# Layer 0 attention: the output product of a slot is placed behind the turning of the probabilities

## The chip, the cores and the metric

One core of a Trainium2 chip runs the whole program. The metric is the time of one execution in microseconds (us) on the device. TensorE (PE in the rows) does matrix products, VectorE (DVE), ScalarE (ACT) and GpSimd (POOL) do the elementwise work, SyncE (SP) issues transfers. Each engine works through its own queue of instructions in order and waits at semaphores that other engines raise.

## The reference, cut to what matters

The model has two layers, each made of a conditioned attention and a conditioned feed-forward part. The change is in the attention of layer 0, for 4 batches of 512 positions and 16 heads of width 128:

```
q, k, v = (y @ Wq, y @ Wk, y @ Wv), split into heads; q, k = rope(q), rope(k)
o = o_cmp * g_cmp + o_slc * g_slc + o_swa * g_swa      # three softmaxes over the same scores
x = x + o.reshape(b, n, H * HD) @ Wo
```

The input y of each layer comes from a two-way recurrence over the sequence (a "unit" of it is one batch and one chunk of 128 channels), which VectorE computes as scans between the heads' work.

## The kernel before, in words

The function `layer0_attn` works through 4 x 16 = 64 heads, all 512 positions of one at a time. The three softmaxes of a head are joined into one matrix of probabilities, `pt`, so a head takes these steps:

- `project_v` (L1018, 48 products of f16, into the bank `ps_v`) and `project` (L1009, 24 products, q and k into `ps_q`);
- `rope`: VectorE (L1205) and ScalarE (`swap`, L869 and L870) read `ps_q`, GpSimd joins them;
- `scores` (L1028, L1030, L1034) into the three banks `ps`;
- `softmax` on VectorE (first instruction L1220, last four L1257) with the exponentials on ScalarE; its last instruction raises the semaphore `p`;
- `turn` (L1046, 10 transposes of 128 x 128 on TensorE, back into `ps`), copied out by ScalarE into `tt_` (L912, three copies, semaphore `t_sb`);
- `values` (L1056, 8 products of f32, into `ps_o`), the probabilities with v;
- `output` (L1078): for each group of four heads and each quarter `co` of the output's columns, 12 products of f16 into `ps_v`, which VectorE adds to `acc` (L1278, semaphore `acc`).

TensorE's queue is written out by a loop over 66 slots, p = 0 to 65. Slot p handles several heads at once, each at another step: `scores(p - 2)`, `project_v(p - 1)`, `project(p)`, `output(p - 6)`, `turn(p - 2)`, `values(p - 2)`, in this order. A slot therefore begins with the scores of a head and ends with the values of the same head, and the softmax of that head has to be made while TensorE does the products between. The bank `ps_v` is used by `project_v`, emptied by ScalarE (`take_v`), then used by `output` and emptied by VectorE; `project_v` of the next slot waits for that.

VectorE has the same loop: the softmax of head p - 2, with a piece of recurrence work in its middle (`between`), the two rope instructions, then `acc` for `output(p - 6)`, then what the slot's place in a group of four, i = p % 4, asks for: after a slot with i = 1 a `log_sum` (L310), after one with i = 2 a `condition` (L314). A slot with i = 1 or i = 3 begins with two backward scans (L294) ahead of its softmax. ScalarE's loop has `swap(p, 0)`, the copies of `turn`, `swap(p, 1)` in this order.

The lines of TensorE's loop that the change touches:

```
for p in range(LAST):
    ...
    if p < HEADS:
        project(p)
    if output_of(p) is not None:
        pe.wait_ge(s["v_sb"], min(p, HEADS))
        output(output_of(p))
    ...
    if p >= 2:
        turn(p - 2)
        values(p - 2)
```

Of the kernel before, what the change touches and what calls it, by code (L numbers as in the profile page):

```python
# [89 lines left out]
def turned_columns(m):  # L90

    return {0: (0, 0), 1: (1, 0), 3: (1, 384), 2: (2, 0)}[m]
# [298 lines left out]
def layer0_attn(k):  # L391
# [7 lines left out]
    HEADS = B * H0  # L399
    GROUPS = B * CC  # L400
    with ExitStack() as ctx:
        def sb(n, s, dt=F32):
# [52 lines left out]
        s = {n: k.sem("a0_" + n) for n in (  # L455
            "const", "wraw", "w64", "whi", "w_ready0", "w_ready1", "w_kept0", "w_kept1", "rot", "wg_loaded", "wg64", "wg_hi", "wg_lo",
            "x_loaded", "sig_step", "sig", "lsum", "inv", "yf", "yhi", "ylo", "gates_raw", "gates_step",
            "gates_sig", "gates", "qproj", "cosed", "swapped", "roped", "q_sb", "ksum", "q_hi", "k_hi", "qk_lo", "vproj", "v_sb", "scores",
            "nmax", "expd", "cmp_step", "cmp_e", "coef", "p_step", "p", "turned", "t_sb", "pv", "of", "o_hi", "o_lo",
            "router", "y", "logits_ps", "logits", "wo_raw0", "wo_raw1", "wo64", "wo_hi", "wo_lo", "out_ps", "acc", "zeroed")}  # L460
# [8 lines left out]
        def cols(t, j, lo=0, hi=None):  # L469

            bank, c0 = score_columns0(j)
            hi = P * (j + 1) if hi is None else hi
            return t[bank][:, c0 + lo:c0 + hi] if isinstance(t, list) else t[:, bank, c0 + lo:c0 + hi]
# [44 lines left out]
        def slot_of(p):  # L518

            return p // H0, p // G, p % G  # L520
# [5 lines left out]
        def output_of(p):  # L526

            return p - (G + 2) if p >= G + 2 else None
# [31 lines left out]
        with nc.Block() as block:  # L560
# [218 lines left out]
            def _(act):  # L779
# [143 lines left out]
                for p in range(LAST):  # L923
# [19 lines left out]
                    if i == 1 and has_next(p):  # L943
                        nb, _, n = next_at(it)
                        wkv.act_log(act, next_unit(it), 0, nb, n, 0)
# [36 lines left out]
            def _(pe):  # L982
                PARTS = ((0, 0), (0, 1), (1, 0))

                def gates(b):

                    if b:
                        pe.wait_ge(s["acc"], output_of(b * H0 + 1) + 1)
                    else:
                        pe.wait_ge(s["v_sb"], 1)  # L990
                    for t in range(TT):
                        at = TILE_SLOT[t] * 48
                        for c in range(CC):
                            for n, (yp, wp) in enumerate(PARTS):
                                mm = pe.matmul(psv[:, at:at + 48], y16[b % 2][:, yp, c, t * P:(t + 1) * P],
                                               wg16[:, wp, c, :], start=c + n == 0, stop=c == CC - 1 and n == 2)
                    mm.then_inc(s["gates_raw"], 1)
# [15 lines left out]
                def project_v(g):  # L1013
                    b = g // H0
                    for t in range(TT):
                        for c in range(CC):
                            for m, (yp, wp) in enumerate(PARTS):
                                mm = pe.matmul(psv[:, t * D0:(t + 1) * D0], y16[b % 2][:, yp, c, t * P:(t + 1) * P],  # L1018
                                               w16[:, g % 2, wp, 2, c, :], start=c + m == 0, stop=c == CC - 1 and m == 2)
                    mm.then_inc(s["vproj"], 1)  # L1020

                def scores(g):
                    pe.wait_ge(s["qk_lo"], g * 2 + 2)
                    for bank, tiles in BANK_TILES0:
                        for j in tiles:
                            lead = NBLK if bank else 0
                            for m, (qp, kp) in enumerate(PARTS):
                                pe.matmul(cols(ps, j, -lead), q16[:, g % 2, qp, j * P:(j + 1) * P],  # L1028
                                          k16[:, g % 2, kp, NBLK - lead:NBLK + P * (j + 1)], start=m == 0, stop=False)
                            mm = pe.matmul(cols(ps, j, P * j), k.ident_b[:], k.causal_b[:],  # L1030
                                           start=False, stop=True)
                        if bank == 1:
                            for m, (qp, kp) in enumerate(PARTS):
                                mm = pe.matmul(ps[1][:, 0:NBLK], q16[:, g % 2, qp, 3 * P:4 * P], k16[:, g % 2, kp, 0:NBLK],  # L1034
                                               start=m == 0, stop=m == 2)
                        mm.then_inc(s["scores"], 1)

                def turn(g):

                    for bank, tiles in ((0, (0,)), (1, (1, 3)), (2, (2,))):  # L1040
                        if bank == 0:
                            pe.wait_ge(s["p"], g * TT + TT)
                        for m in tiles:
                            _, c0 = turned_columns(m)
                            for j in range(m, TT):
                                mm = pe.transpose(ps[bank][:, c0 + (j - m) * P:c0 + (j - m + 1) * P],  # L1046
                                                  cols(pt, j, m * P, (m + 1) * P), k.ident[:])
                        mm.then_inc(s["turned"], 1)

                def values(g):  # L1050
                    for n, m in enumerate((0, 1, 3, 2)):
                        bank, c0 = turned_columns(m)
                        if n == 0 and g:
                            pe.wait_ge(s["of"], g)
                        pe.wait_ge(s["t_sb"], g * 3 + bank + 1)
                        mm = pe.matmul(pso[:, m * P:], v[:, g % 2, m, :], tt_[:, bank, c0:c0 + T - m * P],  # L1056
                                       start=n == 0, stop=n == TT - 1)
                    mm.then_inc(s["pv"], 1)

                def output(n):  # L1060

                    group, co = divmod(n, CC)
                    c = group % CC
                    if co == 0:
                        pe.wait_ge(s["o_lo"], group * G + G)
                        if group < CC:
                            pe.wait_ge(s["wo_lo"], group * G + G)
                    if n:
                        pe.wait_ge(s["acc"], n)
                    output_heads(n, 0, G)  # L1070

                def output_heads(n, lo, hi):

                    group, co = divmod(n, CC)
                    c = group % CC
                    for h in range(lo, hi):
                        for m, (op, wp) in enumerate(PARTS):
                            mm = pe.matmul(out_bank(n), wo16[:, wp, c, h, co * P:(co + 1) * P], o16[:, group % 2, op, h, :],  # L1078
                                           start=h + m == 0, stop=h == G - 1 and m == 2)
                    if hi == G:  # L1080
                        mm.then_inc(s["out_ps"], 1)
# [10 lines left out]
                for p in range(LAST):  # L1092
                    b, it, i = slot_of(p)
                    if p % H0 == 2 and p < HEADS:
                        gates(b)
                    if p >= 2:
                        scores(p - 2)
                    if 1 <= p <= HEADS:
                        if output_of(p - 1) is not None:
                            pe.wait_ge(s["acc"], output_of(p - 1) + 1)  # L1100
                        if p % H0 == 2:
                            pe.wait_ge(s["gates_step"], b * 2 + 1)
                        project_v(p - 1)
                    if p < HEADS:
                        project(p)
                    if output_of(p) is not None:
                        pe.wait_ge(s["v_sb"], min(p, HEADS))
                        output(output_of(p))
                    if p == HEADS + 1:
                        pe.wait_ge(s["swapped"], HEADS * 2)  # L1110
                        pe.wait_ge(s["o_lo"], HEADS - 1)
                        output_heads(OUTPUTS - 4, 0, G - 1)
                    if p >= 2:
                        turn(p - 2)
                        values(p - 2)
                for n in (OUTPUTS - 3, OUTPUTS - 2):
                    output_heads(n, 0, G - 1)
# [10 lines left out]
            def _(dve):  # L1128
# [152 lines left out]
                for p in range(LAST):  # L1281
                    b, it, i = slot_of(p)
                    if i == 1 and has_next(p):
                        nb, _, n = next_at(it)
                        for m in range(2):
                            wkv.dve_backward(dve, next_unit(it), nb, n, m)
# [1725 lines left out]
```

## Time and profile before

| what | value |
|---|---|
| median of 3 runs (lowest, highest) | 2194.34 us (2188.91, 2197.18) |
| the profiled execution | 2195.33 us |
| its span, first to last instruction | 2193.6 us |
| TensorE busy, share of the span | 1919.4 us, 87% |
| VectorE busy | 1594.1 us, 73% |
| ScalarE busy | 1364.2 us, 62% |
| GpSimd busy | 1112.0 us, 51% |
| mean granted clock of TensorE | 0.950 of full speed |

The profiled execution's own time is 1.7 us over its span and 1 us over the median of the runs. Busy shares are means over all stages; the slots of layer 0 take the first half of the span, from about 82 us to 1137 us.

### The profile page before, as it was taken

What the parts mean: (1) busy time and instruction counts of PE and PEld (TensorE: products, weight loads), DVE (VectorE), ACT (ScalarE), POOL (GpSimd) and SP (SyncE); (2) the same over time, 40 slices, a digit from 0 to 9 for tenths busy, and PEclk for the clock granted to TensorE, in tenths of its full rate; (3) what the DMA queues carried; (4) which work ended last, traced back from release to release, by engine and by line L of the source; (5) the groups of instructions that cost most, each with busy time, mean ns of one, the idle gap of its engine ahead of it and who ended that gap; (6) DMA issues with size and microseconds to landing.
All of it is one profiled execution on the core that took longest, in us unless ns stands there. A gap on an engine that the chain in (4) does not pass through costs nothing. (4 is left out here: it accounts for less than half of the span.)

```text
span 2193.6 us, 40174 instructions
## 1 busy us (share of the span) xinstructions
PE 1919.4 (87%) x14497; PEld 1197.4 (55%) x14497; DVE 1594.1 (73%) x3508; ACT 1364.2 (62%) x3321; POOL 1112.0 (51%) x868
## 2 busy tenths in 40 slices
PE   0789999999999999999984999656899888878999
PEld 0456566666656666666664555334556566633444
DVE  7799988888878886888741789546778787734770
ACT  6578776776777777777741343255768686745442
POOL 5677677677667676566613466433223222200540
PEclk9899999999999999999985999878999999889999
DMA  4334432322223222443116644454324243335100
GB/s 175 128 111 135 127 107 76 109 72 81 75 88 101 71 85 83 130 145 118 52 58 260 263 145 148 181 183 131 131 92 147 91 138 128 121 125 190 36 24 19
DMA packets 110977, 256.72 MB, mean 117 GB/s; under 512 B 10944, under 2 KB 39744, under 8 KB 108736
## 3 DMA queue, kind: packets, MB, share of 16 engines
q1 hardware_dynamic: 91520, 204.92, 28.1%
q10 hardware_dynamic: 16704, 40.90, 5.3%
q0 software_dynamic: 2560, 8.39, 1.0%
q8 instruction: 114, 1.87, 0.4%
q14 instruction: 79, 0.65, 0.1%
HBM read 175.79 MB, written 75.24 MB: 114 GB/s over the span
## 5 line engine op out<-in xcount | busy, mean ns | idle before, releaser
L1009 PE MATMUL ps_q<-a_y,a_w 128*128 128x512 f16 x1536 | 343.9, 381 | 57.5 <-POOL a_y L704 57.1
L1009 PEld LDWEIGHTS ps_q<-a_y,a_w 128*128 128x128 f16 x1536 | 147.8, 98 | 225.4 <-issue 60.1
L727 POOL TENSOR_TENSOR a_rb<-a_rb,router_y 128x512 f32<-128x512 f32 x128 | 181.0, 1414 | 167.1 <-ACT a_rb L870 166.4
L1220 DVE TENSOR_REDUCE a_nmax<-ps_s 128x1 f32<-128x512 f32 (+3 forms) x256 | 123.5, 483 | 106.7 <-PE ps_s L1030 106.5
L1018 PE MATMUL ps_v<-a_w,a_y 128*128 128x128 f16 x3072 | 183.1, 220 | 0.0
L869 ACT ACTIVATE a_rb<-ps_q 64x512 f32<-64x512 f32 x128 | 76.0, 593 | 170.4 <-DVE a_ra L1205 168.8
L1056 PE MATMUL ps_o<-a_tt_,a_v 128*128 128x512 f32 (+3 forms) x512 | 158.4, 453 | 24.4 <-ACT a_tt_ L912 21.1
L1018 PEld LDWEIGHTS ps_v<-a_w,a_y 128*128 128x128 f16 x3072 | 175.4, 98 | 1.2
L1078 PE MATMUL ps_v<-a_o,a_wo 128*128 128x512 f16 x732 | 168.0, 379 | 1.9 <-ACT a_v L896 1.9
L889 ACT ACTIVATE ps_s<-ps_s,a_nmax 128x512 f32<-128x512 f32 (+3 forms) x256 | 125.2, 489 | 39.4 <-DVE a_nmax L1222 39.3
L2167 ACT ACTIVATE a_t<-ps 128x512 f16<-128x512 f32 (+1 forms) x192 | 88.0, 525 | 88.7 <-PE ps L2358 79.4
L1028 PE MATMUL ps_s<-a_k,a_q 128*128 128x512 f16 (+3 forms) x768 | 134.0, 304 | 8.3 <-POOL a_k L738 8.3
L736 POOL TENSOR_TENSOR a_q<-a_q 128x512 f16<-128x512 f32 x64 | 75.5, 1180 | 127.3 <-ACT a_q L903 127.3
L2160 ACT ACTIVATE a_ef<-ps,a_nmax 128x512 f32<-128x512 f32 (+3 forms) x256 | 131.7, 537 | 11.7 <-DVE a_nmax L2513 10.3
L1056 PEld LDWEIGHTS ps_o<-a_tt_,a_v 128*128 128x128 f32 x512 | 84.3, 195 | 88.0 <-issue 54.2
L214 POOL TENSOR_TENSOR wkv_eukv<-wkv_euk,wkv_kt 128x512 f32<-128x512 f32 x56 | 76.5, 1366 | 107.1 <-DVE wkv_euk L251 107.1
L1250 DVE SCALAR_TENSOR_TENSOR a_pt<-ps_s,a_coef,a_pc 128x512 f32<-128x512 f32 (+3 forms) x256 | 123.3, 544 | 2.2
L2037 POOL TENSOR_TENSOR a_qk<-a_qkf,a_qk 128x512 f16<-128x512 f32 x32 | 37.1, 1161 | 171.2 <-ACT a_qk L2139 94.3
L2858 PE MATMUL psf_e<-f_h,f_w 128*128 128x512 f16 x512 | 112.7, 382 | 10.0 <-ACT w_w L2793 10.0
L1078 PEld LDWEIGHTS ps_v<-a_o,a_wo 128*128 128x128 f16 x732 | 71.5, 98 | 88.0 <-ACT a_v L896 2.1
L2513 DVE TENSOR_REDUCE a_nmax<-ps 128x1 f32<-128x512 f32 (+3 forms) x256 | 107.3, 477 | 9.0 <-PE ps L2348 8.9
L2519 DVE TENSOR_TENSOR a_t<-ps,a_t 128x512 f16<-128x512 f32 (+1 forms) x192 | 103.5, 589 | 11.4 <-ACT a_t L2167 11.0
(327 smaller groups left out, 4963.0 us busy)
## 6 DMA issues: line engine op xcount, KB each, us to landing
a_w<-wqkv_split SPq DMA_DIRECT2D x48, 768.0 KB, 4.7
scratch_numlog<-wkv_nl ACTq DMA_DIRECT2D x40, 512.0 KB, 2.7
wkv_kt<-in_fT ACTq DMA_DIRECT2D x56, 256.0 KB, 2.9
router_y<-in_wqkv SPq DMA_DIRECT2D x16, 768.0 KB, 5.4
wqkv_split<-a_w SPq DMA_DIRECT2D x16, 768.0 KB, 7.0
a_stacks<-qk_parts SPq DMA_DIRECT2D x96, 128.0 KB, 2.6
gate_up<-in_gate_up SPq DMA_DIRECT2D x8, 1408.0 KB, 11.5
a_nlc<-scratch_numlog SPq DMA_DIRECT2D x18, 512.0 KB, 5.0
```

What stands on the lines that cost most here:

```text
L727: pool.tensor_tensor(rb[:, n, :], rb[:, n, :], rot[:, 2 * n + 1, :], ALU.mult).then_inc(s["roped"], 1)
L889: act.activation(cols(ps, j), cols(ps, j), ACT.Exp, bias=nmax[:, 0, j:j + 1], accum_out=sums[:, 1, n:n + 1]).then_inc(s["expd"], 1)
L1009: mm = pe.matmul(psq[n][:], w16[:, g % 2, wp, n, c, :], y16[b % 2][:, yp, c, :], start=c + m == 0, stop=c == CC - 1 and m == 2)
L1018: mm = pe.matmul(psv[:, t * D0:(t + 1) * D0], y16[b % 2][:, yp, c, t * P:(t + 1) * P], w16[:, g % 2, wp, 2, c, :], start=c + m == 0, stop= ...
L1028: pe.matmul(cols(ps, j, -lead), q16[:, g % 2, qp, j * P:(j + 1) * P], k16[:, g % 2, kp, NBLK - lead:NBLK + P * (j + 1)], start=m == 0, sto ...
L1056: mm = pe.matmul(pso[:, m * P:], v[:, g % 2, m, :], tt_[:, bank, c0:c0 + T - m * P], start=n == 0, stop=n == TT - 1)
L1078: mm = pe.matmul(out_bank(n), wo16[:, wp, c, h, co * P:(co + 1) * P], o16[:, group % 2, op, h, :], start=h + m == 0, stop=h == G - 1 and m ...
L1220: dve.tensor_reduce(nmax[:, 0, j:j + 1], cols(ps, j), AX, ALU.max, negate=True)
L1250: dve.scalar_tensor_tensor(out=cols(pt, j).rearrange("p (m n) -> p m n", n=BLK), in0=cols(ps, j).rearrange("p (m n) -> p m n", n=BLK), sca ...
L2160: act.activation(cols(ef[:, i % 2], j), cols(ps[i % 2], j), ACT.Exp, bias=nmax[:, i % 2, j:j + 1], accum_out=sums[:, i % 2, j:j + 1]).then ...
L2513: m = dve.tensor_reduce(nmax[:, i % 2, j:j + 1], cols(ps[i % 2], j), AX, ALU.max, negate=True)
L2858: mm = pe.matmul(pse[co % 2][:], w1[:, part, co, n, :], h[:, n, :], start=n + part == 0, stop=n == NF - 1 and part == 1)
```

## The change

`output` of a slot is issued between `turn` and `values` instead of ahead of `turn`. No instruction is added or removed, and the waits of each step stay with it.

```
                     if p < HEADS:
                         project(p)
-                    if output_of(p) is not None:
-                        pe.wait_ge(s["v_sb"], min(p, HEADS))
-                        output(output_of(p))
                     if p == HEADS + 1:
                         pe.wait_ge(s["swapped"], HEADS * 2)
                         pe.wait_ge(s["o_lo"], HEADS - 1)
                         output_heads(OUTPUTS - 4, 0, G - 1)
                     if p >= 2:
                         turn(p - 2)
+                    if output_of(p) is not None:
+                        pe.wait_ge(s["v_sb"], min(p, HEADS))
+                        output(output_of(p))
+                    if p >= 2:
                         values(p - 2)
```

This is TensorE's queue in the second half of a slot in the steady state, before (`a0_p`, `a0_t_sb`, `a0_acc` are the semaphores named above; `ident` is the unit matrix of the transposes):

```order
L1009 MATMUL ps_q<-a_y_0,a_w 128x512 [waits a0_swapped]
L1009 MATMUL ps_q<-a_y_0,a_w 128x512 x11
L1078 MATMUL ps_v<-a_o,a_wo 128x512 [waits a0_acc,a0_v_sb]
L1078 MATMUL ps_v<-a_o,a_wo 128x512 x11
L1046 MATMUL ps_s<-ident,a_pt 128x128 [waits a0_p]
L1046 MATMUL ps_s<-ident,a_pt 128x128 x9
L1056 MATMUL ps_o<-a_tt_,a_v 128x512 [waits a0_t_sb,a0_of]
```

And the same place in the changed kernel:

```order
L1009 MATMUL ps_q<-a_y_0,a_w 128x512 [waits a0_swapped]
L1009 MATMUL ps_q<-a_y_0,a_w 128x512 x11
L1046 MATMUL ps_s<-ident,a_pt 128x128 [waits a0_p]
L1046 MATMUL ps_s<-ident,a_pt 128x128 x9
L1078 MATMUL ps_v<-a_o,a_wo 128x512 [waits a0_acc,a0_v_sb]
L1078 MATMUL ps_v<-a_o,a_wo 128x512 x11
L1056 MATMUL ps_o<-a_tt_,a_v 128x512 [waits a0_t_sb,a0_of]
```

The ten transposes, with their wait for the probabilities, now stand directly behind the projections, and the twelve products of `output` stand between them and the values.

On VectorE the order is as it was. This is what stands there around the instruction that takes the output product, in a slot with i = 0 and the start of the next one:

```order
L1257 SCALAR_TENSOR_TENSOR a_pt<-ps_o,a_coef,a_pt 128x128 [waits a0_p_step]
L1205 TENSOR_TENSOR a_ra<-ps_q,router_y 128x512 [waits a0_q_sb,a0_qproj] x2
L1263 SCALAR_TENSOR_TENSOR a_w<-router_y,a_w 128x1536 [waits a0_whi]
L1278 SCALAR_TENSOR_TENSOR a_acc<-ps_v,a_acc 128x512 [waits a0_acc_loaded2,a0_out_ps]
L1268 SCALAR_TENSOR_TENSOR a_wo<-router_y,a_wo 128x512 [waits a0_wo_hi]
L294 SCALAR_TENSOR_TENSOR wkv_bwd<-ps_d,wkv_tail,wkv_fwd 128x512 [waits wkv0_num,wkv0_ln,wkv0_tail]
L294 SCALAR_TENSOR_TENSOR wkv_bwd<-ps_d,wkv_tail,wkv_fwd 128x512
L1220 TENSOR_REDUCE a_nmax<-ps_s 128x1 [waits a0_scores]
```

Nothing moved here; L1278 waits for the product's end (`a0_out_ps`), and the backward scans and the next softmax are queued behind it (L1263 and L1268 are weight work of the first 15 slots only).

## Rows read from the trace of the kernel before

**Rows 1.** Busy in 154:1102: length, PE, PEld, DVE, ACT, POOL, PEclk, DMA, GB/s.

```profile
154.00:1102.00 948.00, 927.53 (x7161) 583.00 (x7160) 797.52 (x2093) 700.84 (x1831) 656.21 (x515) 1.00 0.30 98
```

**Rows 2.** Waits of TensorE in 154:1102: us in total, times, longest.

```profile
PE ps_o L1056 <- ACT a_tt_ L912: 16.3, 32, 1.2
PE ps_s L1046 <- DVE a_pt L1257: 0.9, 1, 0.9
```

**Rows 3.** Timeline of TensorE, slot p = 40 (i = 0): start, us, engine, line.

```profile
714.55 0.81 PE L1028 MATMUL ps_s<-a_k,a_q 128*128 128x512 f16 x3
...
724.37 2.75 PE L1078 MATMUL ps_v<-a_o,a_wo 128*128 128x512 f16 x12
726.96 1.25 PE L1046 MATMUL ps_s<-ident,a_pt 128*128 128x128 f32 x10
728.48 2.40 PE L1056 MATMUL ps_o<-a_tt_,a_v 128*128 128x512 f32 x8 [0.27 <-ACT a_tt_ L912]
730.72 0.81 PE L1028 MATMUL ps_s<-a_k,a_q 128*128 128x512 f16 x3
```

**Rows 4.** Timeline of VectorE, the same slot.

```profile
715.46 0.69 DVE L1220 TENSOR_REDUCE a_nmax<-ps_s 128x1 f32<-128x512 f32 x1 [3.62 <-PE ps_s L1030]
...
725.55 0.35 DVE L1257 SCALAR_TENSOR_TENSOR a_pt<-ps_o,a_coef,a_pt 128x128 f32<-128x128 f32 x1
...
727.16 0.69 DVE L1278 SCALAR_TENSOR_TENSOR a_acc<-ps_v,a_acc 128x512 f32<-128x512 f32 x1
727.77 2.45 DVE L294 TENSOR_TENSOR_SCAN wkv_bwd<-ps_d,wkv_tail,wkv_fwd 128x512 f32<-128x512 f32 x2
```

**Rows 5.** Timeline of ScalarE, the same slot.

```profile
727.74 1.36 ACT L912 ACTIVATE a_tt_<-ps_s 128x512 f32<-128x512 f32 x3
```

**Rows 6.** Timeline of TensorE, the first products of slots p = 39 and p = 42.

```profile
698.53 0.81 PE L1028 MATMUL ps_s<-a_k,a_q 128*128 128x512 f16 x3
...
746.74 0.81 PE L1028 MATMUL ps_s<-a_k,a_q 128*128 128x512 f16 x3
```

**Rows 7.** Timeline of VectorE and GpSimd, slots p = 38 to 41.

```profile
695.59 1.84 DVE L314 SCALAR_TENSOR_TENSOR a_yf<-wkv_nl,wk_fomd,a_sg 128x512 f32<-128x512 f32 x1
695.61 1.27 POOL L727 TENSOR_TENSOR a_rb<-a_rb,router_y 128x512 f32<-128x512 f32 x1 [3.69 <-ACT a_rb L870]
...
697.35 2.45 DVE L294 TENSOR_TENSOR_SCAN wkv_bwd<-ps_d,wkv_tail,wkv_fwd 128x512 f32<-128x512 f32 x2
...
699.72 0.66 DVE L1220 TENSOR_REDUCE a_nmax<-ps_s 128x1 f32<-128x512 f32 x1
...
709.11 0.35 DVE L1257 SCALAR_TENSOR_TENSOR a_pt<-ps_o,a_coef,a_pt 128x128 f32<-128x128 f32 x1
...
740.99 0.34 DVE L1257 SCALAR_TENSOR_TENSOR a_pt<-ps_o,a_coef,a_pt 128x128 f32<-128x128 f32 x1
```

**Rows 8.** Timeline of VectorE and TensorE, slot p = 4, which has no output product.

```profile
129.34 0.35 DVE L1257 SCALAR_TENSOR_TENSOR a_pt<-ps_o,a_coef,a_pt 128x128 f32<-128x128 f32 x1
...
129.74 1.31 PE L1046 MATMUL ps_s<-ident,a_pt 128*128 128x128 f32 x10 [1.42 <-DVE a_pt L1257]
132.27 2.40 PE L1056 MATMUL ps_o<-a_tt_,a_v 128*128 128x512 f32 x8 [1.22 <-ACT a_tt_ L912]
```

**Rows 9.** Timeline of TensorE, slot p = 11.

```profile
249.44 1.31 PE L1046 MATMUL ps_s<-ident,a_pt 128*128 128x128 f32 x10 [0.94 <-DVE a_pt L1257]
251.98 4.08 PE L1056 MATMUL ps_o<-a_tt_,a_v 128*128 128x512 f32 x8 [1.23 <-ACT a_tt_ L912]
```

**Rows 10.** Busy time during those values, columns as in rows 1.

```profile
252.20:255.60 3.40, 3.40 (x7) 1.77 (x7) 1.73 (x3) 1.58 (x4) 3.32 (x3) 0.50 0.92 217
```

**Rows 11.** Timeline of TensorE, slot p = 65.

```profile
1126.58 2.40 PE L1046 MATMUL ps_s<-ident,a_pt 128*128 128x128 f32 x10 [3.54 <-DVE a_pt L1257]
```

**Rows 12.** Timeline of TensorE and VectorE, slot p = 52 (last batch, i = 0).

```profile
909.83 0.81 PE L1028 MATMUL ps_s<-a_k,a_q 128*128 128x512 f16 x3
...
919.62 0.35 DVE L1257 SCALAR_TENSOR_TENSOR a_pt<-ps_o,a_coef,a_pt 128x128 f32<-128x128 f32 x1
```

More of the change, by code:

```diff
@@ L1105, in _ @@
                         project(p)
-                    if output_of(p) is not None:
-                        pe.wait_ge(s["v_sb"], min(p, HEADS))
-                        output(output_of(p))
                     if p == HEADS + 1:
@@ L1114, in _ @@
                         turn(p - 2)
+                    if output_of(p) is not None:
+                        pe.wait_ge(s["v_sb"], min(p, HEADS))
+                        output(output_of(p))
+                    if p >= 2:
                         values(p - 2)
```

## The prediction, made before the changed kernel ran

> **What bounds the kernel now.** I read the busy time by stage first. In the slots that have both a projection and an output product (p = 6 to 63, 58 slots) TensorE is busy 927.5 of 948.0 us at full granted clock, VectorE 797.5 [rows 1]: TensorE bounds this stage, with 20.5 us of gaps to win at most. The chain of waits says what the gaps are: 16.3 us in 32 waits of the values for ScalarE's copies of the turned probabilities, and only 0.9 us, once, in the turning for the probabilities themselves [rows 2]. So the product that stands between the projection and the turning hides something, and the values are hardly covered.
>
> The timeline of one slot shows what is hidden. I count from the slot's first product, 714.55. The projection is done, and the output product starts, at +9.82; the turning starts at +12.41, the values at +13.93, the next slot at +16.17 [rows 3]. On VectorE the softmax starts at +0.91, when the first scores are there, and its last instruction ends at 725.55 + 0.35 = 725.90, which is +11.35 [rows 4]. The probabilities are thus 1.53 us late for the end of the projection and 1.06 us early for the turning where it now stands. The softmax cannot run ahead: its input is made at the start of the same slot.
>
> **The change, step by step.** No work is added; each slot gets another wait.
>
> The turning, new place. Slot p = 4 has no output product and so already has the order projection, turning: the probabilities end at 129.69 and the turning starts at 129.74, 0.05 later, after 1.42 us without work, and takes 1.31 [rows 8]. I take 0.05 and 1.31 for the new slots.
>
> The product, new place. It takes 2.75 us, and each run's end as shown lies 0.16 beyond the start of the next (724.37 + 2.75 against 726.96) [rows 3]. The values' wait goes: without cover it is 1.22 us [rows 8], now there are 2.59 us of product. ScalarE's three copies take 1.36 us and end 3.2 us after the probabilities (727.74 + 1.36 against 725.90) [rows 4, 5]; the values will start 0.05 + 1.31 + 2.75 - 0.32 = 3.79 us after them, so nothing waits.
>
> The slot's new length is then the end of the probabilities plus 0.05 + 1.31 + 2.75 + 2.40 - 3 x 0.16 = 6.03 us. For i = 0: 11.35 + 6.03 = 17.38 against 16.17, +1.21. For i = 2 the rows repeat: +1.2. For i = 1 (p = 41) the end is 741.33 - 730.72 = +10.61 [rows 3, 7], so 16.64 against 746.74 - 730.72 = 16.02 [rows 6], +0.62. For i = 3 (p = 39) it is 709.46 - 698.53 = +10.93, so 16.96 against 16.02, +0.94 [rows 3, 6, 7].
>
> What is late next: VectorE's take of the product, and what is queued behind it. After the probabilities it does two rope instructions and then waits for the product, which will end 0.05 + 1.31 - 0.16 + 2.75 = 3.95 us after them; L1278 follows 0.04 later, and the instruction behind it starts 0.61 after that [rows 4], at 4.60. The next softmax could start at 6.03 + 0.91 = 6.94. After a slot with i = 0 the two backward scans lie between, 2.37 from start to start (697.35 to 699.72) [rows 7]: 6.97, just late, +0.03. After one with i = 2 there is `condition` too, 1.76 from start to start [rows 7]: 8.73, so 1.79 late, where it is now 699.72 - 698.53 - 0.91 = 0.28 late [rows 6, 7]. That pushes the softmax of the i = 3 slots back by 1.51 more, and their probabilities with it: 0.94 + 1.51 = +2.45. For i = 1: +0.65.
>
> The duration of `condition` is the uncertain price in this. It took 1.84 us beside a multiplication of GpSimd that began 0.02 us after it [rows 7]; L1278, the same kind of instruction on the same 128 x 512 but with one operand in PSUM, took 0.69 [rows 4]. With 0.69 the push is 1.15 less. GpSimd's multiplication follows ScalarE's swap, which follows the rope, so it keeps its place relative to the probabilities and another piece of it will be running; I take 1.84. The Trainium skill (SBUF — State Buffer, on the port pair that VectorE and GpSimd share) has an exclusive lock for a VectorE instruction with two operands in SBUF against a GpSimd instruction that reads SBUF; the rows agree, as the instruction ends 0.55 us after the multiplication.
>
> Sum of the loop: 15 slots each with i = 2 and 3, 14 each with i = 0 and 1: 15 x 1.2 + 15 x 2.45 + 14 x 1.21 + 14 x 0.65 = 80.8. In the last batch the i = 0 slots have no recurrence of a next batch in their softmax: it ends at 919.97 - 909.83 = +10.14 [rows 12], which would make +0.15 and not +1.21 in four slots; I take 3 off, since VectorE will be late there as well: **78**. The slots p = 64 and 65 wait for their probabilities already (3.54 us in the last [rows 11]); there the product only moves from ahead of that wait to behind it, 2 x 2.59 = **5**.
>
> The clock. The longest new stops are those of i = 3: 10.93 + 1.51 + 0.05 - 9.82 = 2.7 us, 15 times; the others are 0.8 to 1.6. In this stage the granted clock is full [rows 1], but after the two stops of slot p = 11 (0.94 and 1.23 us around a turning) it was 0.50, that is 1.2 GHz, and the values took 4.08 us for 2.40 [rows 9, 10], 1.68 more; slot p = 4 with stops of 1.42 and 1.22 kept 2.40 [rows 8]. So a stop of that order sometimes costs 1.7. I take 9 of the 15: 9 x 1.68 = **15**; the ends are none (0) and all 15 with the two last slots (29). The Trainium skill (TensorE: Matmul & The Clock Gate, on oscillation) speaks against this change: activity holds the clock up, and a loop whose engine stops in every turn can pay for the fall in every turn. By that every slot would pay; slot p = 11 agrees and slot p = 4 does not.
>
> Sum: 78 + 5 + 15 = 98 us on the profiled execution's 2195.3 gives 2293; the runs' median is 1 us lower, which I leave.
>
> **Rivals.** *VectorE is not late.* If `condition` and the scans hid behind TensorE, the i = 3 slots would cost 0.94 only: 15 x 1.51 = 23 less, and their stops would be 1.2 us with few falls: 2195 + 55 + 5 = 2255. VectorE does idle 3.62 us ahead of a softmax [rows 4], which speaks for it; the count of 1.79 us above speaks against.
>
> *The clock holds.* Without falls 2195 + 83 = 2278; slot p = 4 speaks for it, p = 11 against.
>
> *The clock falls in most slots*, the page's case: 58 slots and the two last, 60 x 1.68 = 101; 83 + 101 = 184, 2379 at the extreme. The stops of 0.8 to 1.6 us stand alone in a slot, unlike those of p = 11, so I hold it unlikely.
>
> *The other side: the probabilities are in time.* Then each slot wins the values' waits, 16.3 us [rows 2], and 58 times the 0.16 of overlap, 9.3: 2170. It needs probabilities at +9.8 or earlier; a slot loses from about +10.0 on. The earliest that I found is +10.14 [rows 12], most are 0.5 to 1.3 later, and the softmax, bound to its scores, has no reason to end earlier. That order and waits are as the diff says shows in TensorE's queue, so no change at all needs gain and loss to cancel.
>
> **How the numbers follow.** Forecast (probabilities late, VectorE pushed, some falls) 0.60, 2293; its own range 2278 to 2310. The clock holds 0.15; VectorE not late 0.13; most slots fall 0.08; in time 0.02; cancelled 0.02. With the cheap `condition` and no fall the sum is 83 - 15 x 1.15 = 66, so 2261; the other end, all long stops with falls, is 83 + 29, 2307, and a little of the next case. The range 2258 to 2318 leaves out part of VectorE not late (2255), most of the many falls and the last two. A measurement of this kernel can tell about 0.5%, 11 us. Slower 0.96, within 0.02, faster 0.02.
>
> **What would show it.** In the changed profile TensorE should wait for the probabilities in L1046 in nearly every slot, some 80 to 100 us in all where it was 0.9; the waits of L1056 for ScalarE should be gone; L1278 should wait some 2.6 us for TensorE in every slot; slots should take 17.4, 18.5, 17.4 and 16.7 us for i = 2, 3, 0, 1; the softmax of i = 3 should begin 2.7 us after its slot and not 1.19. The granted clock of the stage should be below 1. I am wrong if the probabilities end earlier in their slot than now, if the i = 3 slots stay under 17.2, or if falls come after stops of 1.4 us.

## The result, and the profile after

The changed kernel takes 2296.34 us (median of 4 runs, 2295.6 to 2299.55) against 2194.12 us (4 runs, 2188.91 to 2197.18). The ratio of the two is 1.0471, with a 95% interval of 1.0449 to 1.0494: it is slower by 102 us, where 98 were forecast. The profiled execution took 2296.71 us with a span of 2295.0; the instructions are the same in number, and the difference lies in the slots of layer 0.

The busy time of the slots p = 6 to 63 of the changed kernel, columns as in [rows 1]:

```profile
154.00:1202.00 1048.00, 952.77 (x7164) 592.95 (x7162) 799.30 (x2093) 700.96 (x1831) 656.01 (x519) 0.97 0.27 89
```

The same work takes 1048 us instead of 948. TensorE's busy time rose by 25 us with the same matrix instructions, and its mean granted clock fell to 0.97; the other 75 us are time in which it does nothing.

The waits of TensorE and the two longest of VectorE in this stretch (us in total, times, longest), which answer to [rows 2]:

```profile
PE ps_s L1046 <- DVE a_pt L1258: 95.2, 58, 3.7
...
DVE a_acc L1279 <- PE ps_v L1078: 175.5, 58, 4.5
DVE a_nmax L1221 <- PE ps_s L1030: 37.0, 26, 2.2
```

The turning waits for the last probabilities in each of the 58 slots, 95.2 us where it was 0.9 once, and the values' waits for ScalarE, 16.3 us before, are gone. VectorE now stands 175.5 us in front of the product that it must take. (VectorE's line numbers are one higher than before, L1258 for L1257.)

The timeline of TensorE shows slots p = 38 (i = 2), 39 (i = 3) and the start of 40: start, us, engine, line, in brackets the idle time before and who ended it.

```profile
735.73 0.81 PE L1028 MATMUL ps_s<-a_k,a_q 128*128 128x512 f16 x3
...
747.13 1.31 PE L1046 MATMUL ps_s<-ident,a_pt 128*128 128x128 f32 x10 [1.41 <-DVE a_pt L1258]
748.27 2.75 PE L1078 MATMUL ps_v<-a_o,a_wo 128*128 128x512 f16 x12
750.87 2.32 PE L1056 MATMUL ps_o<-a_tt_,a_v 128*128 128x512 f32 x8
753.02 0.81 PE L1028 MATMUL ps_s<-a_k,a_q 128*128 128x512 f16 x3
...
765.52 1.41 PE L1046 MATMUL ps_s<-ident,a_pt 128*128 128x128 f32 x10 [2.52 <-DVE a_pt L1258]
766.73 4.38 PE L1078 MATMUL ps_v<-a_o,a_wo 128*128 128x512 f16 x12
770.95 2.32 PE L1056 MATMUL ps_o<-a_tt_,a_v 128*128 128x512 f32 x8
773.11 0.81 PE L1028 MATMUL ps_s<-a_k,a_q 128*128 128x512 f16 x3
```

Each slot stops ahead of L1046, 1.41 us for i = 2 and 2.52 for i = 3, and then runs through. In the second slot the turning and the product, which had stood still before, take 1.41 and 4.38 us and not 1.31 and 2.75: 1.73 more. Slot 38 is 753.02 - 735.73 = 17.29 long, slot 39 is 20.09; before they were 16.16 and 16.02.

The timeline of VectorE in the same stretch, and of GpSimd beside `condition` (L314), which answer to [rows 7]:

```profile
746.73 0.35 DVE L1258 SCALAR_TENSOR_TENSOR a_pt<-ps_o,a_coef,a_pt 128x128 f32<-128x128 f32 x1
...
751.07 0.69 DVE L1279 SCALAR_TENSOR_TENSOR a_acc<-ps_v,a_acc 128x512 f32<-128x512 f32 x1 [2.80 <-PE ps_v L1078]
751.67 1.73 DVE L314 SCALAR_TENSOR_TENSOR a_yf<-wkv_nl,wk_fomd,a_sg 128x512 f32<-128x512 f32 x1
753.33 2.45 DVE L294 TENSOR_TENSOR_SCAN wkv_bwd<-ps_d,wkv_tail,wkv_fwd 128x512 f32<-128x512 f32 x2
755.70 0.66 DVE L1221 TENSOR_REDUCE a_nmax<-ps_s 128x1 f32<-128x512 f32 x1
...
765.13 0.34 DVE L1258 SCALAR_TENSOR_TENSOR a_pt<-ps_o,a_coef,a_pt 128x128 f32<-128x128 f32 x1
...
771.15 0.69 DVE L1279 SCALAR_TENSOR_TENSOR a_acc<-ps_v,a_acc 128x512 f32<-128x512 f32 x1 [4.48 <-PE ps_v L1078]
...
751.58 1.28 POOL L727 TENSOR_TENSOR a_rb<-a_rb,router_y 128x512 f32<-128x512 f32 x1
```

After the rope VectorE waits 2.80 us for the product, and only then come `condition`, the two backward scans and the softmax of slot 39, which starts 755.70 - 753.02 = 2.68 us after its slot (1.19 before). Its probabilities end at +12.45 (10.93 before). In slot 38 they end at +11.35, as before.

The granted clock during the long product of slot 39, columns as in [rows 1], which answers to [rows 10]:

```profile
766.60:770.00 3.40, 3.40 (x11) 1.28 (x9) 0.06 (x1) 3.22 (x7) 2.55 (x3) 0.50 0.39 159
```

It is 0.50, that is 1.2 GHz, after a stop of 2.52 us. In this stage such a fall of the clock is seen 17 times (once before), and each costs 1.44 to 1.74 us.

Set against the slots of before, one by one, the 58 slots are 99.3 us longer, the last two 7.5, the first four 0.3 shorter: 106.5. The span grew by 101.4 only; the other 5 us lie outside these slots, where no instruction was changed.

### The profile page after: what moved, and what is told of

It reads as the page before. It is cut to its first block and busy times, and to the rows that moved or that the text cites. A ratio compares the mean times of both kernels' runs of the same rounds, so it can differ in the third digit from the quotient of the medians.

```text
span 2295.0 us, 40174 instructions
## 1 busy us (share of the span) xinstructions
PE 1944.5 (85%) x14497; PEld 1206.3 (53%) x14497; DVE 1596.1 (70%) x3508; ACT 1364.1 (59%) x3321; POOL 1107.3 (48%) x868
## 5 line engine op out<-in xcount | busy, mean ns | idle before, releaser
L1078 PE MATMUL ps_v<-a_o,a_wo 128*128 128x512 f16 x732 | 191.9, 418 | 0.0
L1046 PE MATMUL ps_s<-ident,a_pt 128*128 128x128 f32 x640 | 93.2, 298 | 111.8 <-DVE a_pt L1258 111.8
L1279 DVE SCALAR_TENSOR_TENSOR a_acc<-ps_v,a_acc 128x512 f32<-128x512 f32 x61 | 42.2, 692 | 187.5 <-PE ps_v L1078 187.5
L1056 PE MATMUL ps_o<-a_tt_,a_v 128*128 128x512 f32 (+3 forms) x512 | 152.8, 442 | 4.5 <-ACT a_tt_ L912 4.5
L1046 PEld LDWEIGHTS ps_s<-ident,a_pt 128*128 128x128 f32 x640 | 75.4, 150 | 143.1 <-DVE a_pt L1258 143.1
L1078 PEld LDWEIGHTS ps_v<-a_o,a_wo 128*128 128x128 f16 x732 | 78.7, 108 | 91.3 <-issue 31.3
```

## The experiments

Three edits of the changed kernel test the three terms of the sum; the rest asks what the old place is worth, and whether a better one exists. "Before" is the kernel before, measured on the same chip as each run. The "take" is VectorE's instruction that adds the product to `acc` (L1279); "steady" are the slots whose lengths repeat every four slots, mainly those of the two middle batches.

**VectorE's queue.** What the take held up is put ahead of it: `log_sum` and `condition`, and the backward scans of the next slot (`backward`, which stood at the start of that slot).

```diff
-                    if output_of(p) is not None:
-                        output(output_of(p))
                     if late_piece(p) is not None:
                         scaled_wo_low(late_piece(p))
...
                     if late_of(p - 2) is not None:
                         late_condition(late_of(p - 2))
+                    backward(p + 1)
+                    if output_of(p) is not None:
+                        output(output_of(p))
```

> The changed kernel, with one change on VectorE: the condition step and the next slot's two backward scans are issued ahead of the instruction that takes the output product, so the late product holds up nothing. If the late product is what pushes the softmax of the i = 3 slots (the prediction's step), that softmax starts 0.9 us after its slot and not 2.7, its probabilities end at about +10.6, the slot takes 10.6 + 6.0 = 16.6 us and not 18.4 to 20.1, its stop is 0.8 us with no clock fall behind it, and the i = 1 slots lose 0.3 us too: 15 x 2.6 + 14 x 0.3 = 43 us less than the changed kernel, about 2253. If the softmax of those slots is late for another reason, the time stays at 2290 to 2300.

It took 2246.93 us (2240.96 to 2247.29), 1.0236 of before (1.0214 to 1.0257), 49 us less than the changed kernel. VectorE in the same place of that kernel, slot 39 starting at 725.20:

```profile
718.90 0.34 DVE L1258 SCALAR_TENSOR_TENSOR a_pt<-ps_o,a_coef,a_pt 128x128 f32<-128x128 f32 x1
...
720.36 0.74 DVE L314 SCALAR_TENSOR_TENSOR a_yf<-wkv_nl,wk_fomd,a_sg 128x512 f32<-128x512 f32 x1
721.02 2.45 DVE L294 TENSOR_TENSOR_SCAN wkv_bwd<-ps_d,wkv_tail,wkv_fwd 128x512 f32<-128x512 f32 x2
723.39 0.66 DVE L1279 SCALAR_TENSOR_TENSOR a_acc<-ps_v,a_acc 128x512 f32<-128x512 f32 x1
726.10 0.69 DVE L1221 TENSOR_REDUCE a_nmax<-ps_s 128x1 f32<-128x512 f32 x1 [2.05 <-PE ps_s L1030]
```

And TensorE there:

```profile
725.20 0.81 PE L1028 MATMUL ps_s<-a_k,a_q 128*128 128x512 f16 x3
...
736.23 1.31 PE L1046 MATMUL ps_s<-ident,a_pt 128*128 128x128 f32 x10 [1.04 <-DVE a_pt L1258]
737.37 2.75 PE L1078 MATMUL ps_v<-a_o,a_wo 128*128 128x512 f16 x12
...
742.12 0.81 PE L1028 MATMUL ps_s<-a_k,a_q 128*128 128x512 f16 x3
```

The softmax starts 0.90 after its slot, and now waits for its scores. The steady i = 3 slots come down from 20.08 to 16.92, and of 17 falls of the clock 2 are left. So the push through VectorE's queue is real, and the falls hang on it. The waits for the probabilities remain:

```profile
153.30:1146.70 993.40, 927.98 (x7164) 583.23 (x7163) 773.98 (x2093) 702.89 (x1831) 652.53 (x519) 1.00 0.29 94
...
PE ps_s L1046 <- DVE a_pt L1258: 65.4, 58, 2.5
```

Which of the moved instructions counts, the next run tells: only `log_sum` and `condition` go ahead of the take, and the scans stay in the next slot.

```diff
-                    if output_of(p) is not None:
-                        output(output_of(p))
                     if late_piece(p) is not None:
...
                     if late_of(p - 2) is not None:
                         late_condition(late_of(p - 2))
+                    if output_of(p) is not None:
+                        output(output_of(p))
```

> The changed kernel with only the condition step (and the log sums) ahead of VectorE's take of the product; the backward scans stay behind it. The push of the i = 3 slots was counted as the condition step's 1.66 us; the scans alone were counted as 0.03 late. So i = 3 should begin its softmax at +1.0 like i = 1, and take 16.9: within 8 us of the run with both moved, 2247 to 2255. If the scans are the larger part of the push, 2270 or more.

2249.18 us (2247.69 to 2249.92), 1.0253 of before (1.0237 to 1.0269), against 1.0236 with the scans ahead too: the softmax of i = 3 starts at +1.02 and the slot takes 16.93. For the i = 3 slots `condition` behind the take is nearly the whole push.

**The clock.** Six products of the same kind, whose result is overwritten, fill part of the stop.

```diff
+                    if output_of(p) is not None and p < HEADS:
...
+                        for m in range(6):
+                            pe.matmul(psv[:], wo16[:, 0, group % CC, 0, 0:P], o16[:, group % 2, 0, 0, :],
+                                      start=m == 0, stop=m == 5)
```

> The changed kernel with six more products of 128 x 512 between projection and turning in the slots p = 6 to 63, which work on operands at hand and whose result is overwritten. They take 1.37 us. If the clock falls come from the length of the stop, the i = 3 stops shrink from 2.7 to 1.3 us and no fall is left in the loop: 17 falls of 1.7 us (29 us) less, and about 6 us more where the probabilities end before the six products do: about 2273. If the falls have nothing to do with the stops, 2296 + 6 = 2302.

2283.73 us (2279.66 to 2290.5), 1.0422 of before (1.0399 to 1.0444): a kernel with 348 more products takes 13 us less. TensorE in its slot 39, which starts at 737.67:

```profile
747.49 1.46 PE L1114 MATMUL ps_v<-a_o,a_wo 128*128 128x512 f16 x6
750.17 1.31 PE L1046 MATMUL ps_s<-ident,a_pt 128*128 128x128 f32 x10 [1.22 <-DVE a_pt L1268]
751.32 2.75 PE L1078 MATMUL ps_v<-a_o,a_wo 128*128 128x512 f16 x12
...
756.06 0.81 PE L1028 MATMUL ps_s<-a_k,a_q 128*128 128x512 f16 x3
```

The probabilities end as late as in the changed kernel (+12.44), but the product takes 2.75 and the slot 18.39: the difference to 20.08, 1.7 us, is the clock alone. 2 falls of 17 are left. The loop became 17.9 us shorter, where 15 falls at 1.7 are 25.5, so the filler took 7.6 back: about 5 where the probabilities were nearly in time, for which 6 were expected, and 2.7 in slots 51 and 59, whose softmax begins later. The gain was smaller than the 23 us expected by the two falls that stayed and this second part, and by the spread of the runs, whose median lies 4 us over the profiled execution (2279.66).

**The lateness of the probabilities.** In the i = 0 and i = 2 slots both forward scans of the recurrence go from the middle of the softmax to behind the rope.

```diff
-                        if i == 0 and has_next(p):
...
-                            wkv.dve_forward(dve, next_unit(it), nb, n)
...
                         rope(p, 1)
+                    if i == 0 and has_next(p):
...
+                        wkv.dve_forward(dve, next_unit(it), nb, n)
...
```

> The changed kernel, with the two forward scans of the i = 0 and i = 2 slots issued behind the probabilities and the rope, where VectorE waits for the output product anyway. If a slot's length is set by the end of its probabilities, these end at +10.1 and not at +11.35 in about 25 slots, and such a slot takes 16.1 and not 17.3: 30 us less, about 2266 (falls of the clock may come elsewhere, 10 us either way). If the slot is set by TensorE or ScalarE and the end of the probabilities only looks like the releaser, the time stays at 2296.

2277.8 us (2275.86 to 2285.37), 1.0396 of before (1.0372 to 1.042). TensorE in slot 38, at 725.67:

```profile
735.87 1.31 PE L1046 MATMUL ps_s<-ident,a_pt 128*128 128x128 f32 x10 [0.21 <-DVE a_pt L1258]
...
741.76 0.81 PE L1028 MATMUL ps_s<-a_k,a_q 128*128 128x512 f16 x3
```

The probabilities end 1.20 us earlier (+10.14), and the slot is 1.20 shorter, 16.09: its length is their end plus 5.95, in this kernel and in the changed one (11.34 and 17.29). The i = 0 and i = 2 slots together give 40 us, four falls of the clock included; the scans, now behind the rope, push the i = 1 and i = 3 slots by 13, falls of the clock (10 in this kernel) included. The expected time was 12 us too low, by that push.

**A part of the product in each place.** Three of the four heads stay ahead of the turning, one goes behind it, so that it covers the values' wait as well. On the kernel before:

```diff
-                        output(output_of(p))
+                        output(output_of(p), 3)
...
                         turn(p - 2)
+                    if output_of(p) is not None:
+                        output_heads(output_of(p), 3, G)
+                    if p >= 2:
                         values(p - 2)
```

> The kernel before with the output product split: three heads ahead of the turning, the fourth behind it, nothing else moved. The turning can start at +11.76, which is behind the probabilities in all slots but a few, so by the step of the late probabilities nothing is lost there; but VectorE takes the product some 1.1 us later. If a later product pushes the i = 3 softmax also in this small form, its probabilities end at about +12.4 and 15 slots take 17.2 for 16.0; i = 1 gains 0.3, i = 0 and 2 nearly nothing (ScalarE's copies wait for swap(p, 0)): about 2204. If cover behind the turning is all that counts, every slot gains 0.28: 2178.

2191.47 us (2185.92 to 2195.52), 0.9983 of before (0.9969 to 0.9997): neither number. The i = 1 slots go from 16.02 to 15.66 and the i = 3 slots to 15.75, but i = 0 and i = 2 stay at 16.16: there ScalarE starts the copies of the turned probabilities at +13.19 as before, so the values cannot start earlier. The push that I had expected did not come in the steady slots either, since `condition` took 0.76 us (in the last batch it did: slots 51, 55 and 59 take 16.9 for 16.02):

```profile
689.82 1.27 POOL L727 TENSOR_TENSOR a_rb<-a_rb,router_y 128x512 f32<-128x512 f32 x1 [3.69 <-ACT a_rb L870]
...
690.88 0.76 DVE L314 SCALAR_TENSOR_TENSOR a_yf<-wkv_nl,wk_fomd,a_sg 128x512 f32<-128x512 f32 x1
```

An earlier run brings the copies forward as well, ahead of ScalarE's first swap, and has the take last (the cut shows the swap alone):

```diff
-                    if p < HEADS:
-                        swap(p, 0)
                     if p >= 2:
                         turn(p - 2)
+                    if p < HEADS:
+                        swap(p, 0)
```

> The kernel before, with the output product split: the products of three heads ahead of the turning, those of the fourth behind it; ScalarE's copies of the turned probabilities ahead of swap(p, 0); and VectorE's take of the product behind the condition step and the next backward scans. By my sum the turning starts at +11.76, when all probabilities but a few are there, the last 0.65 us of the product cover the copies, and a slot takes 15.75 us: 0.28 less in the 29 slots that take 16.02 now and 0.42 in those of 16.17, about 20 us, so 2174. If the values' wait isn't coverable (the copies come as late as before), 2190 to 2195; if the three queues' new order delays something else, over 2195.

2228.86 us (2227.07 to 2234.65), 1.0167 of before (1.0149 to 1.0186): 55 us over my sum, the expectation's last case. The later swap makes GpSimd's rope later, GpSimd's next work is the recurrence's, and VectorE waits for that in the middle of a softmax:

```profile
703.16 1.47 DVE L251 TENSOR_SCALAR wkv_euk<-wkv_ek_raw,wk_eu,wk_cap 128x512 f32<-128x512 f32 x1 [2.40 <-POOL wkv_nl L233]
```

The probabilities of the i = 1 and i = 3 slots end at +13.9 instead of 10.6, and those slots take 17.93. I had costed the move on ScalarE alone. With the swap back in its place, the split and the take last:

> The split of three heads and one, and VectorE's take of the product behind the condition step and the backward scans, with swap(p, 0) in its old place ahead of the copies. If it was the late swap that spoiled the version with the copies first (GpSimd's rope, then its join, then VectorE's euk), the probabilities of i = 1 and 3 end at +10.6 again and these 29 slots take 15.72 for 16.02, the others 16.13 for 16.17: 9 us less than before, 2183. If the take was what spoiled it, over 2220.

2184.82 us (2180.61 to 2190.25), 0.995 of before (0.9931 to 0.997), as expected: it was the late swap. And the take last alone, on the kernel before:

> The kernel before with VectorE's take of the product behind the condition step and the backward scans, as in the run with the change, and nothing else. The i = 3 softmax then starts 0.9 and not 1.19 us after its slot, but its probabilities are 1.5 us early for the turning already: no difference, 2190 to 2194. If this order is worth something by itself, the 50 us that it brought in the changed kernel would partly show here as well (2170 or less).

2191.21 us (2186.62 to 2196.02), 0.9985 (0.9973 to 0.9998): with the product in its old place VectorE's order is worth next to nothing, where in the new place it was worth 49 us.

**The rest of the probabilities' way.** Added to the split with the take last: both forward scans of the i = 0 slots behind the rope,

> The version with the split and the take moved, and also the forward scans of the i = 0 slots behind their probabilities. Those end at +10.1 and not at +11.35, swap(p, 0) and the copies come 1.2 us earlier, and some 11 slots with i = 0 take 15.72 for 16.17: 13 us less than before, about 2178. If VectorE then comes late to the next softmax by more than the 1.1 us that the i = 1 slots have to spare, the gain is gone: 2185 or more.

2191.96 us (2185.23 to 2195.31), 0.9982 (0.9968 to 0.9996): the second case of the expectation. The i = 0 slots take 15.66, but the softmax of the i = 1 slots starts 2.01 after its slot, and they take 16.62. Then the second of the two scans alone, for i = 0 and i = 2:

```diff
-                            wkv.dve_forward(dve, next_unit(it), nb, n)
+                            wkv.dve_forward_ek(dve, next_unit(it), nb, n)
...
                         rope(p, 1)
+                    if i == 0 and has_next(p):
...
+                        wkv.dve_forward_ekv(dve, next_unit(it), nb, n)
```

> The version with the split and the take moved, and the second of the two forward scans of the i = 0 and i = 2 slots (1.2 us, with the small instruction behind it) issued behind the probabilities and the rope. If the end of the probabilities sets when ScalarE swaps and copies, they end at about +10.2 in these slots, the values start at +13.5 and not +13.93, and with one scan only VectorE is back in time for the next softmax: some 26 slots take 15.66 for 16.16, 13 us less than without it, and 24 less than before: about 2170. If VectorE comes late again, as with both scans behind, 2185 or more.

2181.27 us (2179.72 to 2185.7), 0.9943 (0.9929 to 0.9957), between the two numbers. All steady slots take 15.66, but some of the first and the last batch, where VectorE has more to do (p = 7, 9, 11, 15, 51, 55, 59), take 16.9 to 21.2. The same two edits of VectorE with the whole product in the changed kernel's place:

> The changed kernel's place of the product with the same two edits on VectorE (take behind the condition step and the backward scans, second forward scan behind the probabilities). VectorE then pushes nothing and the probabilities end at about +10.2 in i = 0 and 2 and +10.97 in i = 1 and 3. By the prediction's sum of 5.95 a slot still takes 16.15 and 16.92, since the probabilities are never there at +9.8: about 2247 - 28 = 2219, some 25 us more than before. If the place itself costs nothing once VectorE is in order, at most 2195.

2229.34 us (2228.44 to 2234.06), 1.017 (1.0155 to 1.0186), 48 us more than with the split and 10 more than expected: the steady slots are 16.09 and 16.93, as worked out, some of the first batch over 19. Even with VectorE's order made for it, the place behind the turning costs. Last, the split everywhere, and the two edits of VectorE only in p = 16 to 47 (the cut is against the version with both edits everywhere):

```diff
+                    late_take = H0 <= p < 3 * H0
...
+                    if not late_take and output_of(p) is not None:
+                        output(output_of(p))
...
-                    backward(p + 1)
-                    if output_of(p) is not None:
+                    if late_take:
+                        backward(p + 1)
                         output(output_of(p))
```

> The split of the output product in all slots, and the two edits on VectorE (take behind the condition step and the backward scans, second forward scan behind the probabilities) only in the slots p = 16 to 47; in the first batch VectorE has weight work and in the last one the late recurrence work, and there the version with both edits everywhere had i = 3 slots of 16.9 to 21.2. The 32 slots keep their 15.66, 17 us less than before, the others go as in the version with the split alone, near zero: about 2176. If the edits bring nothing beyond the version with the take alone, 2185.

2177.95 us (2176.26 to 2180.8), 0.9933 of before (0.9919 to 0.9947): 15 us faster than before. Its slots p = 6 to 63, and TensorE in one of them:

```profile
154.20:1085.10 930.90, 918.39 (x7164) 583.82 (x7163) 790.91 (x2093) 703.18 (x1831) 656.64 (x516) 1.00 0.31 100
...
693.14 2.11 PE L1078 MATMUL ps_v<-a_o,a_wo 128*128 128x512 f16 x9
695.09 1.25 PE L1046 MATMUL ps_s<-ident,a_pt 128*128 128x128 f32 x10
696.18 0.81 PE L1078 MATMUL ps_v<-a_o,a_wo 128*128 128x512 f16 x3
696.83 2.32 PE L1056 MATMUL ps_o<-a_tt_,a_v 128*128 128x512 f32 x8
```

No idle time stands in brackets any more: nine products cover the probabilities, three the copies. Of 20.5 us of gaps before, 12.5 remain; the rest of the gain is in the busy time, 918.39 for 927.53 us [rows 1].

## Why the prediction was right, and where its sizes were off

The mechanism was the one forecast, but that the sum came out so close (98 for 101.4 of span) is in part luck: one term was 12 us too high, three were 20.5 too low together, and 5 us fell away elsewhere.

**The waits: 43 us, not 55.** The first kernel of the experiments has only these: 44.8 us in the loop, less one fall more than before (1.7). Step by step the rule holds: slot = end of the probabilities + 5.95 (6.03 was worked out; the values take 2.32, not the 2.40 of [rows 3]), steady slots +1.13 for i = 0 and 2 and +0.90 for i = 1 and 3. What was too high is the number of slots to which it applies. I took 3 us off for the last batch and for i = 0 alone; there the i = 3 slots too have early probabilities, and with VectorE's order mended both kinds cost +0.07. Nor did I see that some slots of before were late already: p = 11 took 19.97 there, 17.23 in that experiment.

One cost I had at nothing. I took over the end of the probabilities from the kernel before, but in i = 1 it moved from +10.61 to +10.97. In the first experiment the softmax starts where it did, at +0.90, and one of its last instructions, whose `a_ewn` and `a_pt` both lie in SBUF, takes 1.24 us and not 0.41. These are slot 41 of before and slot 37 of that experiment:

```profile
740.66 0.41 DVE L1257 SCALAR_TENSOR_TENSOR a_pt<-a_ewn,a_coef,a_pt 128x192 f32<-128x192 f32 x1
740.77 1.33 POOL L738 TENSOR_TENSOR a_k<-a_kk,a_k 128x520 f16<-128x520 f32 x1
...
700.32 1.16 POOL L738 TENSOR_TENSOR a_k<-a_kk,a_k 128x520 f16<-128x520 f32 x1
700.46 1.24 DVE L1258 SCALAR_TENSOR_TENSOR a_pt<-a_ewn,a_coef,a_pt 128x192 f32<-128x192 f32 x1
```

Before, GpSimd's instruction began 0.11 us behind it and took 1.33; now it begins 0.14 ahead of it and takes 1.16. Earlier instructions of the softmax give 0.47 of the 0.83 back, and 0.36 remain: with the 0.08 less of the values, the +0.62 that I had for i = 1 becomes +0.90. In i = 3 it hardly shows, because the softmax there starts 0.29 earlier than before. In the changed kernel itself the instruction takes 1.15 in i = 1 and 0.97 in i = 3.

**The push: 29 us, not 23.** In the i = 3 slots it was 23.4, as worked out: softmax at +2.68 (2.7 forecast), slot 18.39 without the clock (18.47 forecast). For the other slots I had almost none; the i = 1 slots lost 3.3 us and the i = 2 slots 2.3 by a late VectorE, in part in the last batch (p = 53 and 61: +1.71, of which 0.65 and 0.63 remain with the take last). The uncertain price, `condition`, was 1.73 for the 1.84 that I took, and the rival in which VectorE is not late is refuted by the start of the softmax and by two experiments.

**The clock: 27 us, not 15.** 17 falls and not 9, 12 of them in i = 3 slots, the others in p = 9, 18, 34, 50 and 58. In the changed kernel 17 of the 20 stops of 2.08 us or more were followed by a fall, and none of the 38 shorter ones, of which 1.41 us is the usual length; so falls after stops of 1.4, which I had named as a sign of error, did not come. This is a count and no limit: in the kernel before the clock fell after stops of 0.94 and 1.23 us [rows 9], and with the filler it did not after one of 2.46 us (p = 11). The filler shows that the stop is the cause: with the same late probabilities and TensorE at work in half of the stop, 2 falls were left. The Trainium skill (TensorE: Matmul & The Clock Gate, on oscillation) says that a loop which stops in every turn can pay in every turn; the trace agrees for the long stops, which pay every fourth slot, and not for the 1.41 us stops. That the same stop of 2.51 us was followed by a fall in p = 34 and not in p = 18 of the first experiment stays unexplained, and so does why 17 fell and not 9.

**The last two slots: 7.5 us, not 5.** The product moved behind a wait as said, but the clock fell too, where I had reckoned with full speed. TensorE in slots 64 and 65, to be read against [rows 11]:

```profile
1212.20 2.40 PE L1046 MATMUL ps_s<-ident,a_pt 128*128 128x128 f32 x10 [5.39 <-DVE a_pt L1258]
1214.39 4.13 PE L1078 MATMUL ps_v<-a_o,a_wo 128*128 128x512 f16 x12
...
1230.70 2.35 PE L1046 MATMUL ps_s<-ident,a_pt 128*128 128x128 f32 x10 [5.26 <-DVE a_pt L1258]
1232.84 3.44 PE L1078 MATMUL ps_v<-a_o,a_wo 128*128 128x512 f16 x12
```

In slot 64 turning and product take 2.47 us more than the usual 1.31 and 2.75, in slot 65 the product 0.69 more; its turning was slow before as well.

**Outside the slots: 5 us less, not forecast.** No cause was found. In the experiments' profiles the same difference between the slots' sum and the span is -3.5 to +3.2 us, with the same code there, so most of it may be the spread of those stages; that is not shown.

The signs: the turning's waits were 95.2 us (80 to 100 forecast), ScalarE's waits gone, the slots 17.29, 18.39 and the clock, 17.29, 16.92 (17.4, 18.5, 17.4, 16.7). VectorE's wait for the product is 2.80 us in steady slots (2.6 forecast) and 3.0 on average, as the slow products lengthen it. The rival that ends faster needed probabilities at +9.8; none came before +10.14 in a steady slot, as in [rows 12].

## What to carry to other kernels

A product that stands ahead of a wait is paid for by that wait: before it is moved, count when the awaited operand is ready against the end of what would then precede it, because a wait of 0.9 us in the profile can hide one of 95. Then look at who takes the moved result on an engine that works in order; here what was queued behind the take cost 29 us and the stops that this made longer most of 27 more in clock, and one reordering of that queue gave back half of the loss. Where two waits each need a part of the cover, split the product, and price such an edit in every queue that it delays: the split, with VectorE's order fitted to it, gave 0.7%, and its version that held up one swap on ScalarE lost 1.7% through GpSimd.

## What was not expected of the hardware

`condition`, the same instruction on the same tiles, took 1.84 us, 1.73, 1.27, 0.76 and 0.74 in the steady slots of different kernels. In the four cases with a GpSimd multiplication under way it ended 0.54 to 0.55 us after that: starts and durations added, 697.43 after 696.88 [rows 7], 753.40 after 752.86 in the changed kernel, 742.14 (740.87 + 1.27) after 741.59 (740.32 + 1.27) with both scans behind, 691.64 after 691.09 in the first split. Where none ran, as with the take last (720.36; the multiplication began at 721.15), it took 0.74. So the price of this instruction, where GpSimd's is under way, is what remains of that and 0.55, but not under 0.74, and it can be forecast from the two start times, as I had not done. It also is why no push came with the first split: `condition` began 1.09 us later than in the kernel before and ended as early in its slot. The softmax instruction shown above waited in the same way and ended 0.22 us after GpSimd's. The Trainium skill (SBUF — State Buffer, on the shared port pair) calls this an exclusive lock, which whoever starts first holds for its whole instruction. The rows bear it out, slot 41 of before too, where VectorE began 0.11 us ahead and took its 0.41. One row differs: in [rows 7] GpSimd's instruction began 0.02 us after VectorE's, and it was still VectorE that waited; the profile's GpSimd spans are rough, so this small difference may mean nothing.
